# Attention operands stacked by copies inside SBUF instead of through DRAM, and one sample's projections issued before another's score products

## The reference

```
x = x * s1[:, None, :]
x = (x - mu) * lax.rsqrt(var + EPS_IN)
q = heads(einsum('bsh,oh->bso', x, q_weight) * q_dc[:, None, :])
k = heads(einsum('bsh,oh->bso', x, k_weight) * k_dc[:, None, :])
v_flat = einsum('bsh,oh->bso', x, v_weight) * v_dc[:, None, :] * s2[:, None, :]
attn = softmax(einsum('bhqd,bhkd->bhqk', q, k) * scale, axis=-1)
out = einsum('bhqk,bhkd->bhqd', attn, v).transpose(0, 2, 1, 3).reshape(B, S, H)
out = einsum('bsh,oh->bso', out, w_weight) * w_dc[:, None, :]
skip = einsum('bsh,oh->bso', v_flat, u_weight) * u_dc[:, None, :]
return out + skip
```

## Time and profile before

| | us |
|---|---|
| median of 3 runs | 706.46 |
| lowest and highest of them | 705.04 and 708.86 |
| the profiled execution, its own time | 703.65 |
| its span, first to last instruction | 701.9 |

### The profile page before, as it was taken

How to read it: one execution, slowest core, us unless ns; L and a number is a source line. 1 busy time by engine, 2 the same in 40 slices (tenths; PEclk the granted TensorE clock), 3 DMA queues, 4 the chain that set the end, 5 groups by cost and what they waited for, 6 DMA issues and landing times.

```text
span 701.9 us, 10046 instructions
## 1 busy us (share of the span) xinstructions
PE 505.5 (72%) x3232; PEld 292.8 (42%) x3232; DVE 500.8 (71%) x820; ACT 262.5 (37%) x513; POOL 129.7 (18%) x136
## 2 busy tenths in 40 slices
PE   3657888788888878899992000077777759899888
PEld 3545546365564624689882000011111113233367
DVE  2825858668595775466666897279999979899942
ACT  2315454545545343266763647012212213223211
POOL 5302112020120200150000236103131103222200
PEclk9858999999999998999995555579999989999999
DMA  9745271634607250030000134645445545555441
GB/s 354 232 73 100 37 135 20 119 67 70 121 18 134 47 91 1 2 159 21 1 1 0 67 112 150 102 72 107 100 96 100 101 98 120 117 126 129 105 150 53
DMA packets 44902, 65.06 MB, mean 93 GB/s; under 512 B 19536, under 2 KB 34256, under 8 KB 41152
## 3 DMA queue, kind: packets, MB, share of 16 engines
q1 hardware_dynamic: 41520, 59.26, 37.8%
q0 software_dynamic: 784, 3.15, 1.1%
q10 hardware_dynamic: 2560, 2.16, 0.9%
HBM read 41.88 MB, written 22.61 MB: 92 GB/s over the span
## 4 chain that ended last, share of the span: by engine, by line
DVE 34%; PE 30%; ACT 15%; DMA 11%; issue 5%; SPq 2%; POOL 2%; DVEq 0%; ACTq 0%
DVE zst L1363 19%; ACT ex L529 7%; PE bank L707 7%; DVE acc L1225 5%; DMA bst<-bd_d 4%; PE bank L726 4%; DMA qst<-mT 3%; DVE mx L1165 3%; ACT acc L569 2%; PE bank L763 2%; PE bank L955 2%; PE bank L965 2%; PE bank L1051 2%; PE bank L736 2%; PE bank L746 2%
## 5 line engine op out<-in xcount | busy, mean ns | idle before, releaser
L1363 DVE CUSTOM_DVE_ANT_0 zst<-zst,bank,hi 128x512 f32<-128x512 f32 x256 | 191.5, 748 | 33.6 <-PE bank L955 25.0
L955 PE MATMUL bank<-xst,bst 128*128 128x512 bf16 x256 | 87.6, 402 | 94.1 <-DMA bst<-bd_d 61.5
L637 ACT ACTIVATE yb<-bank,ybias 128x512 f32<-128x512 f32 x64 | 44.0, 687 | 177.2 <-PE bank L965 166.8
L955 PEld LDWEIGHTS bank<-xst,bst 128*128 128x128 bf16 x256 | 24.7, 98 | 177.3 <-DVE zst L1363 110.7
L1165 DVE TENSOR_REDUCE mx<-bank 128x2 f32<-128x512 f32 x128 | 80.0, 685 | 22.5 <-PE bank L726 21.6
L529 ACT ACTIVATE ex<-bank 128x512 f32<-128x512 f32 x128 | 66.4, 619 | 41.4 <-PE bank L736 22.2
L965 PE MATMUL bank<-zst,cst 128*32 128x512 f32 x512 | 70.0, 619 | 0.7 <-DVE zst L1363 0.7
L1183 DVE TENSOR_TENSOR esum<-ex 128x1024 f32<-128x1024 f32 x32 | 39.1, 1223 | 39.4 <-ACT ex L529 39.4
L1225 DVE SCALAR_TENSOR_TENSOR acc<-xrp,wcv,acc 128x256 f32<-128x256 f32 x96 | 40.1, 481 | 29.3 <-ACT acc L569 28.7
L867 PE MATMUL bank<-xres,win 128*128 128x256 f32 x256 | 57.6, 382 | 1.2 <-ACT gateT L574 0.7
L707 PE MATMUL bank<-xnT,w 128*128 128x256 f32 x192 | 52.3, 422 | 4.8 <-ACT xnT L476 4.8
(11 more groups left out here) (169 smaller groups left out, 690.6 us busy)
## 6 DMA issues: line engine op xcount, KB each, us to landing
qk_d<-part SPq DMA_DIRECT2D x64, 96.0 KB, 2.5
xs_d<-xpart SPq DMA_DIRECT2D x16, 384.0 KB, 2.6
xst<-xs_d SPq DMA_DIRECT2D x32, 192.0 KB
xst<-xs_d SPq DMA_DIRECT2D x32, 128.0 KB
y_d<-yb SPq DMA_DIRECT2D x128, 32.0 KB
ytk<-y_d SPq DMA_DIRECT2D x16, 256.0 KB, 3.6
bst<-bd_d SPq DMA_DIRECT2D x32, 102.0 KB
qst<-qk_d SPq DMA_DIRECT2D x8, 384.0 KB, 4.6
```

What stands on the lines that cost most here:

```text
L637: nc.scalar.activation(yb[:, par, g, :], bank[4 + n % 2][:, :], ACT.Identity, bias=ybias[:, bass.ds(i * (2 * CH // 4) + n, 1)]).then_inc(s ...
L955: mm(bank[k][:, :], bst[:, par, step, :], xst[:, par, step, :], start=True, stop=True)\
L1363: v._custom_dve(bass.dve_ops.TENSOR_ADD_SAT, out=zst[:, t % ZR, :], in0=zst[:, (t - 1) % ZR, :], in1=bank[t % 4][:, :], s0=hi[:, t:t + 1], ...
```

## The change

`qk_d` and `pw` go. SP copies each of the six blocks of q and of k from `part` straight to its place in `qst` or `kst`: 12 DMAs of 128 KB, each from 128 partitions of 1 KB to 16 partitions of 8 pieces of 1 KB. So that one partition of the source holds what one piece of the destination needs, the q and k weights' output columns are permuted on the way in (`by_row`). ACT waits, before it fills `part` again, for the copies themselves. And in sample 0, all four stages of `next_qkv` stand ahead of `early_maxima`.

```diff
-            def stack(b, par, turn, first):
+            def stack(b, par):
                 sp.wait_ge(s["part_ready"], b * 2 + 2)
-                if not first:
-                    sp.wait_ge(s[f"ld_q{par}"], turn * 48)
-                    sp.wait_ge(s[f"ld_k{par}"], turn * 48)
-                for hh in range(NH // HT):
-                    sp.dma_start(qk_d[par, :, :, :, hh * HT:(hh + 1) * HT, :].rearrange("w k d h s -> d (w k) (h s)"),
-                                 part[hh * HD:(hh + 1) * HD, :, :, :].rearrange("p w k s -> p (w k) s"))\
-                      .then_inc(s["pw"], 16)
-                sp.wait_ge(s["pw"], b * (16 * NH // HT) + 16 * NH // HT)
+                if b >= 2:
+                    sp.wait_ge(s["st_done"], b * NH - NH)
                 for w, name, st in ((0, "q", qst), (1, "k", kst)):
-                    if not first:
-                        sp.wait_ge(s["st_done"], b * NH - NH)
-                    at = 0
-                    for run in (3, 2, 1):
-                        src = qk_d[par, w, 0:run] if w == 0 else qk_d[par, w, 3 - run:3]
-                        sp.dma_start(st[at:at + run * HD, par, :, :], src.rearrange("k d h s -> (k d) h s"))\
+                    for at, k in enumerate((0, 1, 2, 0, 1, 0) if w == 0 else (0, 1, 2, 1, 2, 2)):
+                        sp.dma_start(st[at * HD:(at + 1) * HD, par, :, :].rearrange("d (hh o) s -> d hh (o s)", o=HT),
+                                     part[:, w, k, :])\
                           .then_inc(s[f"ld_{name}{par}"], 16)
...
                     if not first:
                         act.wait_ge(s["part_ready"], b * 2)
-                        act.wait_ge(s["pw"], b * (16 * NH // HT))
+                        for n in "qk":
+                            act.wait_ge(s[f"ld_{n}{(b - 1) % 2}"], (b + 1) // 2 * 96)
...
                 if first:
+                    for stage in range(4):
+                        next_qkv(stage)
                     early_maxima(b, par, 0)
                 for n in range(EARLY, NH):
-                    if n == 4:
+                    if first:
+                        pass
+                    elif n == 4:
                         next_qkv(0)
                         next_qkv(1)
...
+    by_row = np.arange(H).reshape(HT, P // HD, HD).transpose(0, 2, 1).reshape(-1)
+    w5[:, :2] = w5[:, :2][..., by_row]
```

## The result

| | us |
|---|---|
| kernel before, median of 6 runs | 707.66 |
| changed kernel, median of 6 runs | 727.67 |
| ratio, with 95% interval | 1.0296 (1.027 to 1.0321) |
| profiled execution before / after, own time | 703.65 / 725.69 |

The forecast was 707.0, no change, with a range of 701.5 to 715. The change costs 20 us. One of the four executions of `e11_staged`, further down, took 1243.72 us where the other three took 740.1 to 742.91, and its ratio goes without it.

What follows compares the result with a forecast made beforehand. The chain was spread thin (recurrence's DVE step 19%), with `m_row` waited for in every sample. +1.5 - 0.6 - 0.4 = +0.5 us on 703.65 gave 704.15, or 707.0 us in the median's terms, no change; range 701.5 to 715.

Steps and rivals of the forecast that it cites:

- the `m_row` term: Row-maxima DMA, samples 1 to 6: 0.25 us more each beside the copies, +1.5 us, between -4.8 and +11.4.
- The rival: Maxima of each sample held behind SP's queued copies: 1.9 us more in six samples, 716.9 us; chance 0.22.
- Sample 0: Its `m_row` DMA would take 0.4 us less than 2.75, sample 1's copies being mostly through: -0.4 us.
- The step before it: Copies' pace: 168 to 199 GB/s, the slower taken, and 0.45 us of SP's time per copy.
- the operands' landing: Samples 1 to 7: operands already arrive in time for PE, so landing them earlier is worth nothing.
- the margin of 5 us: Stacking: copies land 12 us after `part_ready`, 5 us earlier than now.
- The rival on this: Copies at 84 GB/s take 21.3 us, missing the 17.5 us allowed by 3.8 in six samples: 728; chance 0.08.
- the start: Sample 0: projections ahead of plain scores, done at 49.4, maxima end at 59.9 against 60.52: -0.6 us, between -3.7 and +2.0.

Runs made afterwards that it cites:

- e11_staged: Changed kernel with PE's old order and each copy issued as soon as its part is cast, with no hold for `m_row`; 741.99 us, 1.0481.
- e3: Changed kernel, but SP issues a sample's copies only after the `m_row` DMA of the sample ahead has landed; 728.32 us, 1.0351.
- e8: Changed kernel, with only the k copies held until the `m_row` DMA of the sample ahead has landed; 723.38 us, 1.0211.
- e9: Changed kernel with the `m_row` DMA issued by POOL in POOL's own queue instead of by ACT; 732.88 us, 1.0363.
- e10: Changed kernel with PE's old order, each copy issued once its part is cast, the last six held until `m_row` has landed; 695.23 us, 0.983.
- e4: Kernel before, with the row maxima sent through one more small buffer and DMA, stacking and PE's order untouched; 727.4 us, 1.0302.
- e2: Kernel before with only PE's new order in sample 0, operands still stacked through DRAM; 709.53 us, 1.007.
- e5: Changed kernel without the `m_row` DMA; the maxima enter the scores by a second, accumulating matrix product with a selector; 824.09 us, 1.1635.

## Why the prediction was wrong

**The step that failed is the `m_row` term.** I had worked out that some 0.4 MB, 2 us, would wait on SP's queue when `m_row` is sent, and then took 0.25 us, "nearer to the present 2.6, since the engines are saturated either way and the piece is small". The extra is the backlog itself. In samples 1 to 6 the DMA took 4.61 to 4.89 us instead of 2.54 to 2.61, 12.7 us in sum where I had 1.5; e3, e8, e9, e10 and e11 agree: 1.8 with nothing ahead, 4.3 to 4.8 with 2.4 us of copies issued ahead, 6.6 to 7.5 with all twelve. The reason I gave does not hold: saturated engines are not a backlog. Before, `m_row` also landed just behind the last write issued ahead of it (sample 3: 124.81 and 124.99), but SP issued at the rate at which they moved, and that write, like the others, took 2.6 us. So the order of landing stood in that trace already. That my 2 us of backlog and the 2.1 us of the DMA's growth agree so well is in part luck: I had five copies at 168 to 199 GB/s, and it was four at about 120.

**The rival was right in its mechanism and too small.** It was priced at 716.9 (1.9 us in six samples), with a chance of 0.22. The 2.1 us per sample are its 1.9. Missing were:
- *The clock*: of the 17.4 us between samples 1 and 7, 12.7 are the DMA's; the other 4.7 are, by e4's and the changed kernel's stretches, samples whose final scores ran for some or all of the time at 1.2 GHz after the longer wait. I had written about the clock in sample 0 alone.
- *Sample 0*, where I took -0.4 us on the ground that sample 1's copies were "mostly through" at 60. They were not: the last was issued at 59.6, five of twelve had landed, and `m_row` took 7.20 instead of 2.75, +4.45. The step before it failed too: the copies move about 120 GB/s, not 168, and cost SP 0.65 us each, not 0.45. I had bounded the rate by the two halves replaced and called the lower one the slow end; it was outside.

**Right:** that the operands' landing isn't what bounds samples 1 to 7, so part 1 gains nothing there. That it comes at 12 us was wrong, it is 15, and of the margin of 5 us that I had counted on, 2 are left. The rival on this (a miss of the 17.5 us) did not occur; e3 shows how near it is.

**Right:** the start. PE was through sample 1's projections at 49.2 us (forecast 49.4), and DVE's maxima ended at 59.14 (59.9). The changed kernel's rows, to be held against the earlier trace rows:

```profile
38.97 1.09 PE L686 MATMUL bank<-ident,xnb 128*128 128x128 f32 x4 [1.99 <-issue]
...
40.74 8.48 PE L694 MATMUL bank<-xnT,w 128*128 128x256 f32 x24 [0.69 <-ACT xnT L462]
...
49.48 9.66 DVE L1156 TENSOR_REDUCE mx<-bank 128x2 f32<-128x512 f32 x16 [10.61 <-PE bank L713]
```

**The Trainium skill**, by its page DMA: Bandwidth & Descriptors (Queues, rings and completion order): I set its two rules side by side and said that no row told them apart. The runs do. That an engine takes turns between its queues doesn't show: in sample 0 of the changed kernel the packets of `m_row` start 5.21 us after its issue, when nearly all of the copies' pieces have started. That a completion is written only after all earlier writes of that engine on any queue fits the 1.4 to 2.1 us by which it lands behind its own last packet, instead of 0.4. Why its packets wait too, from ACT's queue as from POOL's, stays open.

The Trainium skill's page SBUF — State Buffer (Door 1: The DMA port swizzle) gives 104 GB/s for 16 partitions. The copies' 120 is near that, and far from the 199 of the writes by which I had set the rule aside. Whether the 16 partitions of the destination are what sets the rate, no run here shows, since none varied them.

## What to carry to other kernels

In every run here, a small DMA that something waits for landed only behind what the other queue had issued before it, give or take one issue. So look at what is issued in the few microseconds ahead of it, in bytes and by the rate at which they move, and make the bulk transfer wait for the small one where it has the time; here that made 742 us into 695, where the kernel before took 706. A transfer that is hidden isn't free: making it earlier, simpler or fewer in number can load the stretch in which another one is on the path. And a wait on the matrix engine is to be priced with the clock that it lets fall.

## What the runs showed of the hardware that I had not expected

- Copies within SBUF from 128 partitions to 16, in pieces of 1 KB, move some 120 GB/s with the DMA engines full, below both halves of the way through DRAM (199 and 168 GB/s). Without DRAM in the way the whole stacking took 15 instead of 17 us.
- The hold is the same from two queues (ACT 4.6 us, POOL 4.3 to 4.6), and for loads from DRAM as for copies (8.3 us behind five loads in e2).
- Products over 96 and over 16 partitions by turns, accumulating in one bank, start further apart than products of one kind. PE's rows in e5:

```profile
120.09 0.39 PE L724 MATMUL bank<-mT,sel 16*128 16x256 bf16 x1
120.42 0.39 PE L722 MATMUL bank<-qst,kst 96*128 96x256 bf16 x1
120.74 0.39 PE L724 MATMUL bank<-mT,sel 16*128 16x256 bf16 x1
```

  One starts each 0.32 us, where eight products of the kernel before take 1.05 us together, 0.13 each. Part of this is the clock: the grant is 0.50 from 120 to 124 us although PE is busy in the profile all the time, and at such a grant (e4, 194 to 201 us) eight of one kind take 1.89 us, 0.24 each. 64 products by turns in the place of 32, with the lower clock for all the rest, made a sample 14.6 us longer. Whether the turns or something else in this edit keep the grant down was not tried.
